# One block for the first feed-forward and the second attention, with waits on the query parts in place of the block's end

## The chip, the core and the metric

The kernel runs on one core of a Trainium2 chip. The metric is the device time of one execution, in microseconds (us). TensorE is called PE, VectorE DVE, ScalarE ACT, GpSimd POOL and SyncE SP, as in the profile. SP computes nothing here; it issues nearly all DMAs.

## What is computed

The reference is a gated cross-attention network of four layers on `x` (2 x 256 rows of 512), each added to `x` through a tanh gate:

```
x = x + tanh(g_xattn[0]) * L0_xattn(layernorm(x), ctx)
x = x + tanh(g_ffn[0])   * L0_ffn(layernorm(x))
x = x + tanh(g_xattn[1]) * L1_xattn(layernorm(x), ctx, ctx)
x = x + tanh(g_ffn[1])   * L1_ffn(layernorm(x))
```

The two layers in the middle matter here. `L0_ffn` is a squared-ReLU feed-forward (512 to 1024 to 512) with a latent expert, routed by the two largest gate logits, and a layernorm behind it. `L1_xattn` is an attention with 32 query heads and 8 key/value heads of dimension 16:

```
q = (query @ Wq) -> 32 heads of 16;  k, v = (ctx @ Wk, ctx @ Wv) -> 8 heads of 16, each for 4 query heads
probs = softmax(q k^T / 4);  out = (probs v) @ Wo
```

## The kernel before

The program is three blocks, one behind the other: the first attention (`attn0`), the first feed-forward (`ffn0`), and the second attention together with the second feed-forward (`attn1`, class `Ffn1`). Each block has one instruction stream per engine, written out by hand; within a block, engines meet at semaphores only. At a block's end every engine waits until all five have come to their end.

`ffn0` (L691 to L1080) also prepares the second attention. Its keys and values come first (`pe_k`, `pe_v`). Its queries come last, at the end of the PE stream: for each batch half `b` the rows of `x` are normalised by DVE (`normalise_1`, L868), transposed by PE, copied to `xnT1` by ACT, and multiplied with `wq1` in four tiles `m` (L1078, 4 matmuls each) into the PSUM banks of `qbank[b][m]`. ACT copies a product's high part to `qpart` (L974) and counts `q_hi`; DVE forms the low part (L895) and counts `q_lo`, from 1 to 8. SP stores both parts of each tile to `q_scratch` in DRAM (L797, 2 DMAs a tile, 16 in all) and, after tile 1 of each half, loads the queries of the first turn back in another layout, 8 DMAs each half (L804), into `a_qS`. The first half's loads count on `stack_in[0]`, the second's on `late_in[0]`. In the second half ACT's copy waits until the first half's tile is stored (`q_out[m]`).

`attn1` (L1317 to L1558) runs over 4 turns `i` of two key heads each, and in each turn over 8 units `m` (batch half times 4 query heads), 32 units in all. For a unit PE does, in two halves:

- scores (L1484): 2 matmuls a half, queries by keys, into three PSUM banks `a_score` in turn. DVE takes the negative maximum of each (L1436, four reduces a unit, `s_max`), and PE waits for the reduce of the bank that it writes next.
- transposed scores (L1495, 4 matmuls), then the negative maxima added by a matmul against a rounded identity `a_ident_r` (L1501, 4 matmuls, which wait for all four maxima of the unit), into `a_scoreT`. ACT takes the exponential (L1405).
- from unit 2 on, in one half of the two, the product with the values (L1517, 16 matmuls) into `a_obank`; every second unit, a small transpose (L1526).

The order on PE is `scores(m+1, 0)`, `scores_T(m, 0)`, product with the values, `scores(m+1, 1)`, `scores_T(m, 1)`. Before the first unit DVE rounds the identity (L1425) and copies the value columns `a_vcol` (`windows`, L1430), which POOL has first set to 0 and 1 (L1393, L1395). Unit 4 (second batch half) waits for `late_in[0]`, unit 8 (turn 1) for `stack_in[1]`. SP loads `wo` (L1372, 4 DMAs), waits for `q_out`, loads turn 1 (L1607 and L1378, 16 DMAs), then the second feed-forward's weights, and turn `i` once turn `i-2` is done.

The PSUM banks: `ffn0` has eight of one bank each, `f_bank0` to `f_bank7`. `attn1` allots `a_score0` to `a_score2` first (banks 0 to 2), then the two `a_scoreT` of two banks each (3 to 6) and `a_obank` (7). The query products of the second half lie in banks 0, 1, 2 and 4, the first half's third in bank 5, the transposes' in 0, 1, 6 and 7:

```
    qbank = [[bank[2], bank[4], bank[5], bank[3]], [bank[0], bank[1], bank[2], bank[4]]]
    tr1_bank = [bank[0], bank[1], bank[6], bank[7]]
```

Of the kernel before, what the change touches and what calls it, by code (L numbers as in the profile page):

```python
# [25 lines left out]
P = 128  # L26
# [23 lines left out]
class Shared:  # L50
    pass

# [638 lines left out]
def ffn0(nc, S, ctx, A):  # L691
# [71 lines left out]
    pe_q, q_hi, q_lo = sem("a_pe_q"), sem("a_q_hi"), sem("a_q_lo")  # L763
# [3 lines left out]
    with nc.Block() as block:  # L767
        @block.sync
        def _(sp):
            def load(c):  # L770
                if c >= 3:
                    sp.wait_ge(w_split, c - 2)
                sp.dma_start(staged(c), chunks[c][1].rearrange("(t p) n -> p t n", p=P)).then_inc(slot_in[c % 3], 16)
            sp.dma_start(gate_stage[:], A.gate_w.rearrange("(t p) n -> p t n", p=P)).then_inc(w_in["gate"], 16)
            for c in range(3):
                load(c)
            sp.dma_start(gamma[:], A.ln_gamma.partition_broadcast(P)).then_inc(w_in["affine"], 16)
            sp.dma_start(beta[:], A.ln_beta.partition_broadcast(P)).then_inc(w_in["affine"], 16)
            for c in range(3, 5):
                load(c)  # L780
            for b in range(B):
                sp.wait_ge(k_lo, b + 1)
                for r in range(2):
                    sp.dma_start(S.k_dram[r, :, b * SC:(b + 1) * SC], f32(S.part[b][:, r, :])).then_inc(S.k_out, 16)
            sp.wait_ge(S.k_out, 64)
            for s in range(2):
                S.load_k(sp, 0, s)
            for c in range(5, len(chunks)):
                load(c)
            sp.wait_ge(w_split, len(chunks))  # L790
            sp.dma_start(S.wqo_stage[:], A.wq1.rearrange("(t p) n -> p t n", p=P)).then_inc(S.wq1_in, 16)
            for b in range(B):
                cols = slice(b * SQ, (b + 1) * SQ)
                for m in range(NQ):
                    sp.wait_ge(q_lo, NQ * b + m + 1)
                    for r in range(2):
                        sp.dma_start(S.q_dram[r, m * P:(m + 1) * P, cols], f32(qpart[:, m, r, :])).then_inc(S.q_out[m], 16)  # L797
                    if m == 1:
                        sp.wait_ge(S.q_out[0], 32 * (b + 1))
                        for s in range(2):  # L800
                            for n in range(4):
                                heads = S.q_dram[n // 2].rearrange("(h d) n -> d h n", d=D1)
                                at = 64 * s + D1 * n
                                sp.dma_start(f32(S.qS[at:at + D1, 0, :, cols]), heads[:, s * GRP:(s + 1) * GRP, cols]  # L804
                                             ).then_inc((S.stack_in, S.late_in)[b][0], 16)

        @block.gpsimd
        def _(pool):
            pool.wait_ge(stats_done, 2 * RT)
            rsqrt_rows(pool, rstd[:], mv[:, :, 1], LN_EPS, S.neg_half[:, 0:RT], rstd_step)  # L810
            pool.wait_ge(gate_split, 1)
            pool.tensor_tensor(gateL[:], gate_stage[:], f32(gateH[:]), ALU.subtract).then_inc(gate_split, 1)
            for c, (_, _, hi, lo) in enumerate(chunks):
                pool.wait_ge(w_hi, c + 1)
                pool.tensor_tensor(lo, staged(c), f32(hi), ALU.subtract).then_inc(w_split, 1)
            for t in range(RT):
                for var, out, done, step in ((mv2, rstd2, stats2_done, rstd2_step),
                                             (S.mv1, S.rstd1, stats3_done, S.rstd1_step)):
                    pool.wait_ge(done, 2 * t + 2)
                    rsqrt_rows(pool, out[:, t:t + 1], var[:, t, 1:2], LN_EPS, S.neg_half[:, 0:1], step, 2 * t)  # L820

        @block.vector
        def _(dve):
            layernorm_stats(dve, S.X, stats, mv, stats_done)
            dve.wait_ge(rstd_step, 2)
            for t in range(RT):
                dve.tensor_scalar(xn[:, t, :], S.X[:, t, :], mv[:, t, 0:1], rstd[:, t:t + 1],
                                  ALU.subtract, ALU.mult).then_inc(xn_done, 1)
            for b in range(B):
                dve.wait_ge(k_hi, b + 1)  # L830
                dve.tensor_tensor(S.part[b][:, 1, :], bank[4 + b][:], f32(S.part[b][:, 0, :]),
                                  ALU.subtract).then_inc(k_lo, 1)
            for t in range(RT):
                dve.wait_ge(xnT_done, t + 1)
                dve.tensor_tensor(xnTL[:, :, t * P:(t + 1) * P], bank[t][:].rearrange("p (k n) -> p k n", k=KT),
                                  f32(xnTH[:, :, t * P:(t + 1) * P]), ALU.subtract).then_inc(xnT_lo, 1)
            for i in range(NL):
                dve.wait_ge(lat_done, i + 1)
                dve.tensor_tensor(latTL[:, i, :], bank[i][:], f32(latTH[:, i, :]), ALU.subtract).then_inc(lat_lo, 1)
            for t in range(RT):  # L840
                dve.wait_ge(logits_done, 1)
                dve.max(top[:, t, :], logits[:, t, :]).then_inc(top_done, 1)
            dve.wait_ge(top_done, RT)
            dve.tensor_tensor(route[:], top[:, :, 0], top[:, :, 1], ALU.add).then_inc(route_done, 1)

            def h_lo_part(i):
                dve.wait_ge(h_hi, i + 1)
                dve.tensor_tensor(hTL[:, i, :], relu[:, i % RT, :], f32(hTH[:, i, :]), ALU.subtract).then_inc(h_lo, 1)
            for i in range(NI):
                dve.wait_ge(relu_done, i + 1)  # L850
                dve.tensor_tensor(relu[:, i % RT, :], relu[:, i % RT, :], relu[:, i % RT, :], ALU.mult).then_inc(h_done, 1)
                if i:
                    h_lo_part(i - 1)
                if i == 1:
                    for e in range(NL):
                        dve.wait_ge(exp_done, e + 1)
                        dve.tensor_tensor(expTL[:, e, :], bank[6 + e][:], f32(expTH[:, e, :]), ALU.subtract).then_inc(exp_lo, 1)
            h_lo_part(NI - 1)
            dve.wait_ge(route_done, 1)
            dve.wait_ge(w_in["affine"], 32)  # L860

            def tile_stats(x, stats_t, mv_t, done, base):
                dve.bn_stats(stats_t, x).then_inc(done, 1)
                dve.wait_ge(done, base + 1)
                dve.bn_aggr(mv_t, stats_t).then_inc(done, 1)
# [783 lines left out]
```

## Time and profile before

| what | us |
|---|---|
| median of 3 runs | 1049.95 |
| lowest and highest of them | 1046.86 and 1050.12 |
| time of the profiled execution | 1048.5 |
| its span in the profile | 1046.7 |
| PE busy | 988.8 (94%) |
| DVE busy | 630.4 (60%) |
| ACT busy | 501.2 (48%) |
| POOL busy | 355.3 (34%) |

The first three rows are times of the whole execution; the span is from the first to the last instruction of the profiled one, 1.8 us less than its time. The profile's times are counted from the span's start. The block of `attn0` lasts to about 755, that of `ffn0` to 857.8, the last to the end. A busy PE is not a PE at its peak, since its matmuls overlap, and their ends are modelled.

### The profile page before, as it was taken

To read this page: it belongs to the slowest core of one execution; us is meant where nothing else is said; L and a number is where in the kernel's file an instruction comes from. 1 tells how busy PE (TensorE), PEld (TensorE's weight loads), DVE (VectorE), ACT (ScalarE), POOL (GpSimd) and SP (SyncE) were. 2 spreads that over 40 slices of the span, in tenths; PEclk is the share of its full clock that TensorE was granted. 3 is DMA by queue.
4 is the path that set the end of the run, shared out by engine and by line. 5 is a ranking of instruction groups with operands and counts; after the bars stand their busy time and mean duration, and the time that the engine had idled before them with its cause. 6 is when DMAs were issued, how large, how long until landed. Compare 5 with 4: busy or idle time off the path is not lost. (4 is left out here: it accounts for less than half of the span.)

```text
span 1046.7 us, 18230 instructions
## 1 busy us (share of the span) xinstructions
PE 988.8 (94%) x6748; PEld 853.7 (82%) x6748; DVE 630.4 (60%) x1102; ACT 501.2 (48%) x968; POOL 355.3 (34%) x244
## 2 busy tenths in 40 slices
PE   4899999999999999999999999999999969999975
PEld 3879989898998989899898989989877757666554
DVE  6566457556646755664675566467448736777464
ACT  4357336535634643563464366346345115556423
POOL 3344324424432442533344153331246203500050
PEclk9989999999999999999999999999999988999987
DMA  6011002001100300110030011000053056430001
GB/s 221 1 62 41 2 1 100 0 0 60 40 0 0 100 0 0 60 40 0 0 100 0 0 60 60 0 0 2 19 194 108 14 167 161 61 61 1 2 0 41
DMA packets 31460, 46.53 MB, mean 44 GB/s; under 512 B 3520, under 2 KB 15424, under 8 KB 31424
## 3 DMA queue, kind: packets, MB, share of 16 engines
q1 hardware_dynamic: 30848, 46.03, 14.8%
q8 instruction: 24, 0.39, 0.2%
q14 instruction: 12, 0.10, 0.0%
q10 hardware_dynamic: 576, 0.00, 0.0%
HBM read 41.83 MB, written 4.19 MB: 44 GB/s over the span
## 5 line engine op out<-in xcount | busy, mean ns | idle before, releaser
L432 DVE TENSOR_TENSOR ptL<-tbank,ptH 128x512 fp32r<-128x512 f32 x192 | 132.1, 688 | 82.7 <-ACT ptH L292 82.5
L292 ACT ACTIVATE ptH<-tbank 128x512 fp32r<-128x512 f32 x192 | 115.6, 602 | 91.2 <-PE tbank L544 90.7
L544 PE MATMUL tbank<-ident,probs 128*128 128x128 f32 x864 | 131.0, 276 | 5.3 <-DVE qTL L434 2.8
L318 ACT ACTIVATE probs<-score,negmax 128x768 f32<-128x768 f32 x128 | 115.5, 903 | 29.7 <-DVE negmax L445 29.7
L445 DVE TENSOR_REDUCE negmax<-score 128x1 f32<-128x768 f32 x128 | 118.8, 948 | 14.6 <-PE score L74 14.6
L72 PE MATMUL obank<-ptH,vH 128*128 128x256 f32 x384 | 121.4, 316 | 0.0
L544 PEld LDWEIGHTS tbank<-ident,probs 128*128 128x128 f32 x864 | 97.8, 140 | 14.5 <-DVE probs L411 3.0
L403 DVE TENSOR_REDUCE sumsq<-probs 128x2 f32<-128x256 f32 (+1 forms) x80 | 42.0, 526 | 112.0 <-ACT probs L287 71.8
L74 PE MATMUL score<-wkvH,kvT_lo 128*128 128x256 f32 x384 | 108.7, 283 | 0.0
L73 PE MATMUL score<-wkvL,kvT_hi 128*128 128x256 f32 x384 | 108.7, 283 | 0.0
L72 PE MATMUL score<-wkvH,kvT_hi 128*128 128x256 f32 x384 | 108.6, 283 | 0.0
L74 PE MATMUL obank<-ptH,vL 128*128 128x256 f32 x384 | 108.4, 282 | 0.0
L73 PE MATMUL obank<-ptL,vH 128*128 128x256 f32 x384 | 108.1, 282 | 0.0
L200 POOL TENSOR_TENSOR rnorm<-sumsq,neg_half 128x2 f32<-128x2 f32 (+1 forms) x80 | 71.4, 895 | 107.1 <-DVE sumsq L405 107.0
L205 POOL TENSOR_TENSOR oTL<-o_norm,oTH 128x512 fp32r<-128x512 f32 x32 | 41.3, 1292 | 187.9 <-ACT oTH L312 187.9
L1436 DVE TENSOR_REDUCE a_negmax<-a_score 128x1 fp32r<-128x512 f32 x128 | 82.1, 684 | 32.5 <-PE a_score L1484 32.0
L72 PE MATMUL score<-kTH,qTH 128*128 128x512 f32 (+1 forms) x256 | 92.8, 363 | 5.8 <-ACT probs L318 4.9
L1405 ACT ACTIVATE a_exp<-a_scoreT 128x1024 f32<-128x1024 f32 x64 | 65.5, 1024 | 62.1 <-PE a_scoreT L1501 62.1
L74 PE MATMUL score<-kTH,qTL 128*128 128x512 f32 (+1 forms) x256 | 87.1, 340 | 0.0
L73 PE MATMUL score<-kTL,qTH 128*128 128x512 f32 (+1 forms) x256 | 86.9, 340 | 0.0
L72 PEld LDWEIGHTS score<-wkvH,kvT_hi 128*128 128x128 f32 x384 | 73.7, 192 | 0.3
L73 PEld LDWEIGHTS score<-wkvL,kvT_hi 128*128 128x128 f32 x384 | 73.7, 192 | 0.3
(257 smaller groups left out, 2320.0 us busy)
## 6 DMA issues: line engine op xcount, KB each, us to landing
wqo_stage<-in_wq SPq DMA_DIRECT2D x9, 1024.0 KB, 5.6
wqo_stage<-in_wo SPq DMA_DIRECT2D x8, 1024.0 KB, 5.0
wkv_stage<-in_wkv SPq DMA_DIRECT2D x9, 512.0 KB, 6.4
a_qS<-q_scratch SPq DMA_DIRECT2D x24, 128.0 KB, 4.9
ctx_stage<-in_ctxT SPq DMA_DIRECT2D x2, 1024.0 KB, 12.8
kS<-k_scratch SPq DMA_DIRECT2D x32, 64.0 KB, 3.3
q_scratch<-qpart SPq DMA_DIRECT2D x16, 128.0 KB, 1.9
wqo_stage<-in_down_w SPq DMA_DIRECT2D x3, 512.0 KB, 3.5
```

Of the source, the lines that this page charges most:

```text
L72: pe.matmul(out, a[0], b[0], start=start, stop=False)
L73: pe.matmul(out, a[0], b[1], start=False, stop=False)
L74: return pe.matmul(out, a[1], b[0], start=False, stop=stop)
L200: pool.tensor_tensor(rn[:, GRP * it:GRP * it + n], ss[:, GRP * it:GRP * it + n], S.neg_half[:, 0:n], ALU.pow).then_inc(rn_done, 1)
L292: act.activation(out, tbank[c % 2][:], ACT.Copy, scale=scale).then_inc(t_hi, 1)
L318: act.activation(probs[:, m % NP, :], score[m % 2][:, 0:SKV], ACT.Exp, bias=negmax[:, m:m + 1], accum_out=rsum[:, m:m + 1]).then_inc(s_exp, 1)
L403: dve.tensor_reduce(ss[:, a:a + n], sq[:, it % 3, 0:n], AX.X, ALU.add).then_inc(ss_done, 1)
L432: i = dve.tensor_tensor(out, tbank[c % 2][:], f32(hi), ALU.subtract)
L445: dve.tensor_reduce(negmax[:, m:m + 1], score[m % 2][:, 0:SKV], AX.X, ALU.max, negate=True).then_inc(s_max, 1)
L544: i = pe.transpose(tbank[c % 2][:, n * P:(n + 1) * P], block_in, S.ident[:])
L1405: act.activation(expo[:, m % NX, h].rearrange("p s k q -> p (s k q)"), scoreT[h][:], ACT.Exp).then_inc(s_exp, 1)
L1436: dve.tensor_reduce(negmax[:, e % 16:e % 16 + 1], score[e % NB][:], AX.X, ALU.max, negate=True).then_inc(s_max, 1)
```

## The change

`ffn0` and `attn1` no longer open a block each. Each returns its five streams, and `flamingo` opens one block in which every engine runs its stream of `ffn0` and then that of `attn1`. The wait of all engines for all at the end of `ffn0` is gone. In its place PE waits for `q_lo` at four places: 3 before its first scores, 6 and 7 before the first use of each `a_scoreT`, 8 before the first product with the values. `attn1`'s PSUM is allotted in another order: `a_scoreT` lie in banks 0 to 3, `a_obank` in 4, `a_score` in 5 to 7. The rounded identity is made by DVE in `ffn0`, after the first layernorm. DVE takes the first four maxima before it copies the value columns instead of after. The memory of `ffn0` in SBUF is still given back before `attn1` takes its own. The diff, without the lines that only moved to another indentation:

```diff
+class Programs:
+    def __init__(self, sync, gpsimd, scalar, vector, tensor):
+        self.sync, self.gpsimd, self.scalar, self.vector, self.tensor = sync, gpsimd, scalar, vector, tensor
...
-    pe_q, q_hi, q_lo = sem("a_pe_q"), sem("a_q_hi"), sem("a_q_lo")
+    pe_q, q_hi, q_lo = sem("a_pe_q"), sem("a_q_hi"), S.q_lo
...
-    with nc.Block() as block:
-        @block.sync
-        def _(sp):
+    def sync(sp):
...
                 dve.tensor_scalar(xn[:, t, :], S.X[:, t, :], mv[:, t, 0:1], rstd[:, t:t + 1],
                                   ALU.subtract, ALU.mult).then_inc(xn_done, 1)
+        dve.tensor_copy(S.ident_r[:], S.ident[:]).then_inc(S.ident_set, 1)
...
+    return Programs(sync, gpsimd, scalar, vector, tensor)
...
-    ident_r = sb("a_ident_r", [P, P], f32r)
...
-    score = [ps(f"a_score{i}", [P, 512], fp32) for i in range(NB)]
     scoreT = [ps(f"a_scoreT{i}", [P, 1024], fp32) for i in range(2)]
     obank = ps("a_obank", [P, 512], fp32)
+    score = [ps(f"a_score{i}", [P, 512], fp32) for i in range(NB)]
...
-            dve.tensor_copy(ident_r[:], S.ident[:]).then_inc(ident_set, 1)
-
...
+        maxima(0)
             dve.wait_ge(ones_set, 1)
             windows(0)
-            maxima(0)
...
                 if m:
                     pe.wait_ge(s_exp, 2 * (m - 1) + h + 1)
+            else:
+                pe.wait_ge(S.q_lo, KT + 2 + h)
...
                     if w:
                         pe.wait_ge(o_step, 2 * w)
+                else:
+                    pe.wait_ge(S.q_lo, 2 * KT)
...
+        pe.wait_ge(S.q_lo, 3)
             for t in range(2):
                 scores(0, t)
-            pe.wait_ge(ident_set, 1)
+        pe.wait_ge(S.ident_set, 1)
...
-            for phase in (ffn0, attn1):
                 with ExitStack() as c:
-                    phase(nc, S, c, A)
+                first = ffn0(nc, S, c, A)
+            with ExitStack() as c:
+                second = attn1(nc, S, c, A)
+                with nc.Block() as block:
+                    @block.sync
+                    def _(sp):
+                        first.sync(sp)
+                        second.sync(sp)
...
```

On PE, from the last query products (`f_bank<-xnT,wqo_stage`) to the first maxima added, before:

```order
L1078 MATMUL f_bank<-xnT,wqo_stage 128x256 x3
L767 UNCONDITIONAL_BRANCH
L1470 UNCONDITIONAL_BRANCH [waits barrier_Pool_Activation_PE_DVE_SP_release]
L1484 MATMUL a_score<-kS,a_qS 128x512 [waits stack_in0]
L1484 MATMUL a_score<-kS,a_qS 128x512 x2
L1484 MATMUL a_score<-kS,a_qS 128x512 [waits a_s_max]
L1484 MATMUL a_score<-kS,a_qS 128x512 [waits a_s_max,a_ident_set]
L1484 MATMUL a_score<-kS,a_qS 128x512 [waits a_s_max]
L1495 MATMUL a_scoreT<-a_qS,kS 128x256 x4
L1501 MATMUL a_scoreT<-a_ident_r,a_negmax 128x2x128 [waits a_s_max]
```

The same place with the change:

```order
L1079 MATMUL f_bank<-xnT,wqo_stage 128x256 x3
L1477 MATMUL a_score<-kS,a_qS 128x512 [waits stack_in0,a_q_lo]
L1477 MATMUL a_score<-kS,a_qS 128x512 x2
L1477 MATMUL a_score<-kS,a_qS 128x512 [waits a_s_max]
L1477 MATMUL a_score<-kS,a_qS 128x512 [waits a_s_max,a_ident_set]
L1477 MATMUL a_score<-kS,a_qS 128x512 [waits a_s_max]
L1490 MATMUL a_scoreT<-a_qS,kS 128x256 [waits a_q_lo]
L1490 MATMUL a_scoreT<-a_qS,kS 128x256 x3
L1496 MATMUL a_scoreT<-ident_r,a_negmax 128x2x128 [waits a_s_max]
```

No matmul has moved or gone; two branches and the wait for all engines have gone, and waits on `a_q_lo` have come.

On DVE in `ffn0`, from the first layernorm's statistics to the low parts of the keys (`part`) and of the normalised rows (`f_xnTL`), before:

```order
L60 BN_AGGR f_mv<-f_stats 128x2 x3
L827 TENSOR_SCALAR f_y<-x_rows,f_mv,f_rstd 128x512 [waits f_rstd_step]
L827 TENSOR_SCALAR f_y<-x_rows,f_mv,f_rstd 128x512 x3
L831 TENSOR_TENSOR part<-f_bank,part 128x512 [waits k_hi] x2
L835 TENSOR_TENSOR f_xnTL<-f_bank,f_xnTH 128x4x128 [waits f_xnT_done] x4
```

The same place with the change:

```order
L66 BN_AGGR f_mv<-f_stats 128x2 x3
L829 TENSOR_SCALAR f_y<-x_rows,f_mv,f_rstd 128x512 [waits f_rstd_step]
L829 TENSOR_SCALAR f_y<-x_rows,f_mv,f_rstd 128x512 x3
L831 CAST ident_r<-ident 128x128
L834 TENSOR_TENSOR part<-f_bank,part 128x512 [waits k_hi] x2
L838 TENSOR_TENSOR f_xnTL<-f_bank,f_xnTH 128x4x128 [waits f_xnT_done] x4
```

The cast has come in front of the keys' low parts.

On DVE between the two phases, from the last layernorm on, before:

```order
L868 TENSOR_SCALAR f_y<-x_rows,mv,rstd 128x512 [waits rstd1_step]
L895 SCALAR_TENSOR_TENSOR qpart<-f_bank,qpart 128x256 [waits a_q_hi] x8
L767 UNCONDITIONAL_BRANCH
L1423 UNCONDITIONAL_BRANCH [waits barrier_Pool_Activation_PE_DVE_SP_release]
L1425 CAST a_ident_r<-ident 128x128
L1430 COPY a_vcol<-v_rows 128x8x16 [waits a_ones_set]
L1430 COPY a_vcol<-v_rows 128x8x16
L1436 TENSOR_REDUCE a_negmax<-a_score 128x1 [waits a_pe_s] x12
```

The same place with the change:

```order
L871 TENSOR_SCALAR f_y<-x_rows,mv,rstd 128x512 [waits rstd1_step]
L898 SCALAR_TENSOR_TENSOR qpart<-f_bank,qpart 128x256 [waits a_q_hi] x8
L1430 TENSOR_REDUCE a_negmax<-a_score 128x1 [waits a_pe_s] x4
L1424 COPY a_vcol<-v_rows 128x8x16 [waits a_ones_set]
L1424 COPY a_vcol<-v_rows 128x8x16
L1430 TENSOR_REDUCE a_negmax<-a_score 128x1 [waits a_pe_s] x8
```

The wait for all engines and the cast are gone from here, and four of the twelve reduces have moved ahead of the copies. On POOL the two memsets of `a_vcol` now follow the last reciprocal root of `ffn0` (L67, L73 with the change) with nothing between, and on SP the loads of `wo` follow the last stores to `q_scratch`.

## Rows read from the trace of the kernel before

**Rows 1.** Who waited for whom, 828 to 872: us in total, times, longest.

```profile
PE a_score L1484 <- PEq L767: 7.1, 1, 7.1
```

**Rows 2.** The timeline of SP, issues only: start, us, line, issue, count.

```profile
843.46 3.62 SPq L804 DMA_DIRECT2D a_qS<-q_scratch  x8
...
851.45 3.86 SPq L804 DMA_DIRECT2D a_qS<-q_scratch  x8
855.36 2.00 SPq L797 DMA_DIRECT2D q_scratch<-qpart  x4
857.75 1.76 SPq L1372 DMA_DIRECT2D a_wo<-in_wo  x4
...
865.18 2.81 SPq L1378 DMA_DIRECT2D a_qS<-q_scratch  x4
```

**Rows 3.** The timeline of all engines, 828 to 872: start, us, instructions, [idle before].

```profile
840.27 0.55 DVE L868 TENSOR_SCALAR f_y<-x_rows,mv,rstd 128x512 f32<-128x512 f32 x1 [1.00 <-POOL rstd L67]
...
841.74 1.04 PE L1071 MATMUL f_bank<-ident,f_y 128*128 128x128 f32 x8
...
843.56 7.14 PE L1078 MATMUL f_bank<-xnT,wqo_stage 128*128 128x256 f32 x32 [0.78 <-issue]
...
851.16 0.42 DVE L895 SCALAR_TENSOR_TENSOR qpart<-f_bank,qpart 128x256 fp32r<-128x256 f32 x1 [0.81 <-ACT qpart L974]
...
857.76 0.95 POOL L1393 MEMSET a_vcol<- 128x1024 f32 x1 [17.52 <-POOLq L767]
...
857.80 1.19 PE L1484 MATMUL a_score<-kS,a_qS 64*128 64x512 f32 x3 [7.09 <-PEq L767]
...
859.23 3.67 DVE L1436 TENSOR_REDUCE a_negmax<-a_score 128x1 fp32r<-128x512 f32 x6
...
862.31 1.22 PE L1501 MATMUL a_scoreT<-a_ident_r,a_negmax 128*128 128x256 f32 x4
```

**Rows 4.** The same view from 870 on, after the clock has risen.

```profile
872.78 0.50 PE L1484 MATMUL a_score<-kS,a_qS 64*128 64x512 f32 x2
...
873.31 2.60 DVE L1436 TENSOR_REDUCE a_negmax<-a_score 128x1 fp32r<-128x512 f32 x4 [1.04 <-PE a_score L1484]
...
874.10 0.50 PE L1484 MATMUL a_score<-kS,a_qS 64*128 64x512 f32 x2
...
889.14 0.50 PE L1484 MATMUL a_score<-kS,a_qS 64*128 64x512 f32 x2
```

**Rows 5.** Issue to landing, first-turn queries (L804), then second-turn queries (L1378).

```profile
DMA to landing us min/median/max: 2.0/2.3/2.3
...
DMA to landing us min/median/max: 4.9/5.6/6.3
```

**Rows 6.** Stretches: us, then PE, PEld, DVE, ACT, POOL busy (count), PE's clock, DMA share, GB/s.

```profile
853.00:854.00 1.00, 0.00 (x0) 0.00 (x0) 0.00 (x0) 0.00 (x0) 0.00 (x0) 0.75 0.48 145
...
870.00:871.00 1.00, 1.00 (x9) 0.70 (x7) 0.47 (x4) 0.53 (x1) 0.00 (x0) 0.71 1.09 166
...
983.00:988.00 5.00, 3.21 (x41) 1.93 (x41) 1.00 (x4) 1.41 (x2) 0.00 (x0) 1.00 0.02 3
...
1007.00:1011.00 4.00, 3.78 (x19) 3.58 (x20) 3.90 (x7) 2.38 (x3) 2.15 (x4) 0.57 0.00 0
```

**Rows 7.** L827 (min/median/max ns), timeline of POOL, DVE, PE from 763 on, then L1425.

```profile
L827 DVE TENSOR_SCALAR f_y<-x_rows,f_mv,f_rstd x4: 539/546/2690, 759.6 to 761.0; 128x512 f32<-128x512 f32 x4
...
763.32 2.59 POOL L815 TENSOR_TENSOR upL<-wqo_stage,upH 128x1024 fp32r<-128x1024 f32 x1
...
763.57 1.27 DVE L831 TENSOR_TENSOR part<-f_bank,part 128x512 fp32r<-128x512 f32 x2
...
768.44 1.29 DVE L835 TENSOR_TENSOR f_xnTL<-f_bank,f_xnTH 128x512 fp32r<-128x512 f32 x2 [2.32 <-ACT f_xnTH L915]
...
769.79 0.39 PE L72 MATMUL f_bank<-f_xnTH,gateH 128*8 128x512 f32 x1 [0.75 <-DVE f_xnTL L835]
...
L1425 DVE CAST a_ident_r<-ident x1: 991/991/991, 857.8 to 857.8; 128x128 fp32r<-128x128 f32 x1
```

More of the change, by code:

```diff
@@ L1341, in attn1 @@
     win = sem("a_win")
-    pe_s, s_max, ident_set = sem("a_pe_s"), sem("a_s_max"), sem("a_ident_set")
+    pe_s, s_max = sem("a_pe_s"), sem("a_s_max")
     pe_sT, s_exp, pe_pv = (sem(f"a_{n}") for n in ("pe_sT", "s_exp", "pe_pv"))
@@ new lines, in sync, with load_q @@
+    def sync(sp):
+        wo_v = A.wo1.rearrange("(i s p r) n -> s p r i n", s=2, p=2, r=P // 4)
+        for s in range(2):
+            for pair in range(2):
+                at = 64 * pair + 32 * s
+                sp.dma_start(wo[at:at + 32, :, :], wo_v[s, pair]).then_inc(wo_in, 16)
+        def load_q(i, s):
+            for n in range(4):
+                heads = S.q_dram[n // 2].rearrange("(h d) n -> d h n", d=D1)
+                at, g = 64 * s + D1 * n, 2 * i + s
+                sp.dma_start(f32(qS[at:at + D1, i % 2, :, :]), heads[:, g * GRP:(g + 1) * GRP, :]).then_inc(stack_in[i % 2], 16)
+        for stored in S.q_out:
+            sp.wait_ge(stored, 64)
+        for i in range(1, TURNS):
+            if i >= 2:
+                sp.wait_ge(pe_sT, 2 * NV * (i - 1))
+            for s in range(2):
+                S.load_k(sp, i, s)
+                load_q(i, s)
+            if i == 1:
+                ffn.loads(sp)
+        ffn.sync(sp)
@@ new lines, in gpsimd, with scalar, exp, copy_o @@
+    def gpsimd(pool):
+        pool.memset(vcol[:], 0.0).then_inc(zeroed, 1)
+        pool.wait_ge(zeroed, 1)
+        pool.memset(vcol[:, :, :, :, D1:D1 + 1], 1.0).then_inc(ones_set, 1)
+        ffn.fold(pool)
+        ffn.gpsimd(pool)
+    def scalar(act):
+        def exp(m, h):
+            act.wait_ge(pe_sT, 2 * m + h + 1)
+            if m >= NX and h == 0:
+                act.wait_ge(pe_pv, (m - NX) // 2 + 1)
+            act.activation(expo[:, m % NX, h].rearrange("p s k q -> p (s k q)"), scoreT[h][:], ACT.Exp).then_inc(s_exp, 1)
+        def copy_o(w):
+            act.wait_ge(pe_pv, w + 1)
+            act.activation(o_quad[:, w % 2, :], obank[:, 0:SQ], ACT.Copy).then_inc(o_copied, 1)
+        for m in range(NM):
+            exp(m, 0)
+            if m % 2 == 1 and m >= 3:
+                copy_o((m - 3) // 2)
+            exp(m, 1)
+        copy_o(NW - 1)
+        for t in range(RT):
+            act.wait_ge(pe_t, t + 1)
+            act.activation(oT[:, :, t * P:(t + 1) * P], score[t % 2][:].rearrange("p (k n) -> p k n", k=KT),
+                           ACT.Copy).then_inc(oT_done, 1)
+        ffn.scalar(act)
@@ L1561, in flamingo @@
+    return Programs(sync, gpsimd, scalar, vector, tensor)
 def flamingo(nc, A):
@@ L1600, in flamingo @@
             S.q_dram = nc.dram_tensor("q_scratch", (2, HEADS * D1, ROWS), fp32, kind="Internal").ap()
+            S.q_lo = sem("a_q_lo")
             S.q_out, S.late_in = [sem(f"q_out{i}") for i in range(KT)], [sem(f"late_in{i}") for i in range(2)]
```

886 lines of the change are left out of this document (423 added, 463 removed).

## The prediction

> **What bounds the kernel now.** I read the busy shares first: PE is busy for 94% of the span, so only time in which PE stands still, or runs at its lower clock, can be won. Then the waits between the two phases. PE's longest wait there is the block's end, 7.1 us, named as PE's own sequencer [rows 1]. The timeline tells who was late. PE's last query product ends at 850.71 (the scores start at 857.80 after 7.09 idle), DVE's last low part at 851.16 + 0.42 = 851.58, and POOL has been idle since 857.76 - 17.52 = 840.24 [rows 3]. SP is last: it issues sixteen stores and sixteen loads of queries one after the other, until 855.36 + 2.00 = 857.36, and 0.4 us later the next block begins with `wo` at 857.75 [rows 2]. So four engines wait for a queue of DMA issues, and of these PE needs only the first half's loads at once.
>
> The wait costs more than itself. In the idle time PE's clock falls (0.75 of full between 853 and 854, that is, from 2.4 to 1.2 GHz within that microsecond) and rises again between 870 and 871 [rows 6]. All that PE does from 857.80 to there runs at 1.2 GHz.
>
> **The change, part by part.** The sum is made against the profiled execution, 1048.5 us, and goes by one landmark: the second scores of unit 3, which start at 872.78, when the clock is full again [rows 4].
>
> *The block's end.* PE goes on with the first scores at about 850.7. Of its two waits `q_lo` >= 3 has long been met, and the queries' loads of the first half are issued by 843.46 + 3.62 = 847.08 [rows 2] and land 2.3 us later at the most [rows 5], at 849.4, with 1.3 us to spare. The maxima then wait for DVE, not for PE: DVE's low parts end at 851.58, where the first reduce took until 859.23 to start [rows 3]. First reduce at 851.6: **7.6 us earlier**. The waits on `q_lo` 6, 7 and 8 are met at 851.58 at the latest, before anything that stands behind them could run.
>
> *The clock, and the order on DVE.* From the first reduce to the landmark it took 872.78 - 859.23 = 13.55 us. At the full clock DVE sets the pace here. Four reduces take 2.60 us [rows 4], 0.65 each; the two copies of `a_vcol` take 859.23 - 857.80 - 0.99 = 0.44 [rows 3, 7]. Before the maxima of unit 2 are all there DVE does twelve reduces and two copies, 12 x 0.65 + 0.44 = 8.2 us, until 859.8. Then PE adds them (half of the 1.32 us that lie between two scores without a product, 872.78 to 874.10 [rows 4], so 0.66) and does the first product with the values. Four units take 889.14 - 874.10 = 15.04 [rows 4], 3.76 each; less two halves of 1.32 that leaves 1.1 for the product. The landmark comes at 859.8 + 0.66 + 1.1 = 861.6, that is 10.0 us after the first reduce: **3.6 us less**. PE alone would need about 1.32 for each of these halves, as much as two reduces, so nothing is gained beyond.
>
> *What lies behind.* From the landmark on the order is unchanged and PE was already the bound; all of it comes 11.2 us earlier if its loads are there. Unit 4 needs the second half's queries: issued by 851.45 + 3.86 = 855.31 [rows 2], landed at 857.6, needed at 874.10 - 11.2 = 862.9. Turn 1's last load is issued by 865.18 + 2.81 = 867.99 [rows 2], 0.4 earlier now since SP never stood still for long, and lands 6.3 us later at the most [rows 5], at 873.9; unit 8 needs it at 889.14 - 11.2 = 877.9. SP's queue now has only 4 us of cover where it had 15.
>
> *The cast in `ffn0`.* It costs DVE's queue between 0 and 2.4 us. Alone it is a short operation, at most the 0.99 us of [rows 7], which the idle time of 2.32 ahead of the last two low parts of the rows takes up. But next to POOL such operations are held: one of the four in front of it took 2690 ns, the others about 540, and the cast's own 0.99 us ended at 858.79 right behind POOL's memset, which ran to 858.71 [rows 7, 3]. POOL's next subtraction starts at 763.32 and runs 2.59 us, to 765.91, and the cast would come at 763.57. Held until then, DVE does its four low parts (1.27 + 1.29) until 768.5 or 768.6 and the last two by 769.9, where they ended at 769.73; PE waits for these at 769.79 [rows 7]. I take the held case, which is the nearest row: **0.2 us more**. Without the 2.32 us of idle time it would be 2.4.
>
> *POOL's memset* moves to 840.24, next to DVE's normalisation at 840.27. Between 0 and 0.95 us for DVE; if that operation ends at 841.8 instead of 840.8, it is still ahead of the second four of PE's eight transposes, which started at 841.74 and take 1.04 [rows 3]; DVE's first low parts and SP's stores then come up to 0.95 later, which leaves 0.3 of the 1.3 us above. I take 0.
>
> *The PSUM banks* cost nothing by themselves: they only decide on which `q_lo` each first write waits. With the old order the first score bank would be that of a late query product.
>
> Sum: 1048.5 - 7.6 - 3.6 + 0.2 = 1037.5. The median of the runs is 1.45 above the profiled time, and the four times average 1048.9; against that average it is 1037.9. I predict **1038.0**.
>
> **The rivals.** (a) *The clock falls all the same.* From 850.7 to the first additions at 854.3 PE does three scores, then waits for a reduce before each of the next ones; with the modelled durations it is busy for some 3 of 3.6 us. Then only the 7.6 us remain, since the 13.55 us stay: 1048.5 - 7.6 + 0.2, about 1041; 1039.5 if the clock comes back within 4 us, as it does after 1007 [rows 6]. For it: the clock can stay low while PE is nearly always busy (3.78 of 4 us at 0.57 there). Against it: between 983 and 988 PE is busy for 3.21 of 5 us in small pieces and keeps the full clock [rows 6]. The Trainium skill warns of this (TensorE: Matmul & The Clock Gate, "A second HAM failure mode: psum-queue depth-cycling"): short idle times between groups of matmuls that go round PSUM banks can make the clock swing between its two levels. By that rule the start of the attention is such a place and the time is the 1041 of this rival; the row of 983 to 988 does not bear it out.
>
> (b) *A load takes the place of the barrier.* Turn 1's loads, with 4 us of cover, or the first half's, with 1.3 or less. If turn 1 landed 10 us after its last issue instead of 6.3 it would cost nothing yet; each microsecond beyond is lost in full. 1039 to 1043, say 1041.
>
> (c) *The change doesn't do what it says*: PE's start stays tied to SP's last stores through one of the counts, and only some tenths are won: about 1048.
>
> (d) *Slower.* The place is the same start of the attention: the clock falls there and stays low. A unit of 3.76 us then takes up to twice that. Four such units beyond the landmark lose 15 us, more than the 11.0 won plus the 0.3% (3.1 us) that a measurement of this kernel can tell from no change; that is where it decides. With six it is 1048.5 - 11.0 + 22.6 = 1060. For it: the clock did stay low for 13 us with PE at work from 857.80 on. Against it: that low stretch began in 7 us of idleness, and once up the clock stays up for the rest of this attention.
>
> **How the numbers follow.** Forecast 0.72; (a) 0.15; (b) 0.06; (c) 0.04; (d) 0.03. The forecast's own range is 1036 to 1039.7: 0 to 0.2 for the cast, 0 to 1 for the memset, and the runs' scatter (1046.86 to 1050.12) halved by taking a median. The range reaches on to (a) and most of (b): **1035.3 to 1042**. Faster by over 0.3%: all of the first three, 0.93. Within 0.3%: (c), 0.04. Slower: 0.03.
>
> **What the profile should show.** PE's wait at its first scores gone or below 0.3 us; the first reduce about 8 us earlier relative to the last query product; a clock of 1.00 from there on; the second scores of unit 3 at about 861.6, give or take what the cast moved; no wait of PE before units 4 and 8; SP's issues in one piece up to turn 1's last. The cast at 763.6, ending near 766.0 if held and at 763.8 if not. From unit 3 to the end the profile should be that of before, moved. The prediction is wrong if the granted clock shows 0.5 after 851, if a DMA ends a wait of PE there, or if the time from unit 3 to the end is longer than the 1046.7 - 872.8 = 173.9 us of before by more than 1 us.

## The result and the profile after

The changed kernel took 1040.32 us (median of nine executions, 1036.86 to 1043.88) beside 1047.18 for the kernel before on the same chip (nine, 1043.36 to 1051.33): a ratio of 0.9923, 95% interval 0.9904 to 0.9942, so 6 to 10 us less. The forecast was 1038.0 in a range of 1035.3 to 1042.0. The profiled execution took 1040.32 too, its span 1038.5, against 1048.5 and 1046.7 before.

First the waits of 828 to 872 after the change (us in total, times, longest). They answer to [rows 1]:

```profile
DVE a_negmax L1430 <- PE a_score L1477: 6.1, 6, 1.9
...
ACT qpart L976 <- DMA q_scratch<-qpart: 3.1, 2, 2.7
...
PE a_score L1477 <- DVE a_negmax L1430: 1.4, 2, 1.2
```

PE's 7.1 us at the block's end are gone. What PE waits for now is DVE's maxima. ACT's copies of the query parts wait for stores of the first half. SP's issues, the same view as [rows 2]:

```profile
842.32 1.81 SPq L801 DMA_DIRECT2D q_scratch<-qpart  x4
844.62 3.62 SPq L808 DMA_DIRECT2D a_qS<-q_scratch  x8
848.29 3.85 SPq L801 DMA_DIRECT2D q_scratch<-qpart  x8
852.61 3.86 SPq L808 DMA_DIRECT2D a_qS<-q_scratch  x8
856.51 3.18 SPq L801 DMA_DIRECT2D q_scratch<-qpart  x4
859.74 1.89 SPq L1371 DMA_DIRECT2D a_wo<-in_wo  x4
...
867.31 1.83 SPq L1377 DMA_DIRECT2D a_qS<-q_scratch  x4
```

SP is still busy until 869.14, in one piece, but nobody waits for its end any more. The timeline of all engines, as [rows 3, 4] (start, us, instructions, [idle before]):

```profile
840.74 0.95 POOL L1391 MEMSET a_vcol<- 128x1024 f32 x1
...
840.82 1.14 DVE L871 TENSOR_SCALAR f_y<-x_rows,mv,rstd 128x512 f32<-128x512 f32 x1 [1.00 <-POOL rstd L73]
...
844.11 7.15 PE L1079 MATMUL f_bank<-xnT,wqo_stage 128*128 128x256 f32 x32 [0.78 <-issue]
...
851.19 0.73 PE L1477 MATMUL a_score<-kS,a_qS 64*128 64x512 f32 x3
...
852.08 0.42 DVE L898 SCALAR_TENSOR_TENSOR qpart<-f_bank,qpart 128x256 fp32r<-128x256 f32 x1 [0.35 <-ACT qpart L976]
852.42 2.47 DVE L1430 TENSOR_REDUCE a_negmax<-a_score 128x1 fp32r<-128x512 f32 x4
...
853.16 0.50 PE L1477 MATMUL a_score<-kS,a_qS 64*128 64x512 f32 x1 [1.24 <-DVE a_negmax L1430]
...
853.85 1.00 PE L1477 MATMUL a_score<-kS,a_qS 64*128 64x512 f32 x2 [0.19 <-DVE a_negmax L1430]
...
855.02 1.02 PE L1496 MATMUL a_scoreT<-ident_r,a_negmax 128*128 128x256 f32 x4
...
866.31 0.50 PE L1477 MATMUL a_score<-kS,a_qS 64*128 64x512 f32 x2
...
882.69 0.50 PE L1477 MATMUL a_score<-kS,a_qS 64*128 64x512 f32 x2
```

The scores follow the last query product without a pause. The first reduce starts at 852.42, right behind DVE's last low part. But unit 3's second scores come at 866.31 and not at 861.6. The stretches say why, as [rows 6] (PE, PEld, DVE, ACT, POOL busy, then PE's granted clock):

```profile
852.00:853.00 1.00, 0.00 (x0) 0.00 (x0) 0.92 (x2) 0.05 (x1) 0.00 (x0) 1.00 0.80 273
...
855.00:856.00 1.00, 1.00 (x7) 0.76 (x6) 1.00 (x4) 0.00 (x0) 0.00 (x0) 0.64 0.44 136
860.00:861.00 1.00, 1.00 (x5) 0.78 (x6) 0.39 (x1) 0.32 (x1) 0.00 (x0) 0.50 0.69 203
...
865.00:866.00 1.00, 1.00 (x16) 0.44 (x16) 0.00 (x0) 0.72 (x1) 0.00 (x0) 0.74 1.14 234
```

PE pauses from 851.92 to 853.16, the clock falls to its lower level, 1.2 GHz, between 855 and 856, and is back between 865 and 866. In this execution rival (a) came true.

To compare profiles, whose first feed-forwards start up to 2.6 us apart, I count from the second half's first query product (843.56 before, 844.11 after):

| from ... to | before | after | difference |
|---|---|---|---|
| start of the profile, second half's products | 843.56 | 844.11 | +0.55 |
| ... first reduce | 15.67 | 8.31 | -7.36 |
| ... unit 3's second scores | 13.55 | 13.89 | +0.34 |
| ... first product with `wo` | 117.48 | 116.80 | -0.68 |
| ... end of the span | 56.44 | 55.39 | -1.05 |

The block's end gave its 7.4 us, and the clock's 3.6 us are missing. The last two rows are scatter and no work of the change (over all fourteen profiles they go from 116.8 to 118.2 and from 54.2 to 57.3): in the profile before, PE waits 0.7 us for a copy of the value columns at about 902, and PE is at the lower clock for 25 us in all behind 1000, beside 21 us after.

But nine executions reach from 1036.9 to 1043.9, and they go with the mean granted clock: five at 0.984 or less took 1040.3 to 1043.9, four at 0.986 or more 1036.9 to 1039.1. So the clock may fall in some executions of one and the same program and not in others. That became the question.

The mean clock is a coarse measure for it. Each profile also has low stretches elsewhere, at about 50 to 60 and behind 995. Added up over the span, microsecond by microsecond, PE is at the lower clock at the attention's start and elsewhere for:

| profile | at the start, us | elsewhere, us | mean clock |
|---|---|---|---|
| before | 17 | 31 | 0.978 |
| the change | 10 | 25 | 0.984 |
| change_again | 14 | 32 | 0.979 |
| last_low_part_awaited | 7 | 21 | 0.988 |
| memset_after_normalisation | 0 | 32 | 0.986 |
| one_block_filled | 0 | 27 | 0.988 |

Over all fourteen profiles "elsewhere" goes from 21 to 35 us. By an estimate from these rows that alone makes mean clocks from about 0.984 to 0.991, with nothing at the start. So by this range executions at 0.983 or less fell at the start; from 0.984 to 0.988 the mean doesn't tell.

### The profile page after: what moved, and what is told of

The parts are those of the page before. It is cut to its first block and busy times, and to the rows that moved or that the text cites. A ratio compares the mean times of both kernels' runs of the same rounds, so it can differ in the third digit from the quotient of the medians.

```text
span 1038.5 us, 18220 instructions
## 1 busy us (share of the span) xinstructions
PE 986.1 (95%) x6748; PEld 851.2 (82%) x6748; DVE 628.2 (60%) x1102; ACT 501.7 (48%) x968; POOL 355.5 (34%) x244
```

## The experiments

All twelve in one table. "First reduce" and "to unit 3" are the second and third line of the table above; "pause" is PE's longest between its last query product and the first additions; the last column counts executions at a mean clock of 0.985 or less, and in brackets those at 0.983 or less. The ratio is to the kernel before, run in between on the same chip.

| run | first reduce | to unit 3 | pause | clock low | median us (runs) | ratio, 95% interval | at 0.985 or less |
|---|---|---|---|---|---|---|---|
| before | 15.67 | 13.55 | 7.09 | 853-871 | 1047.18 (9) | 1 | – |
| the change | 8.31 | 13.89 | 1.24 | 855-866 | 1040.32 (9) | 0.9923 (0.9904-0.9942) | 5 (4) |
| change_again | 8.23 | 15.07 | 1.17 | 854-869 | 1041.53 (6) | 0.9907 (0.9878-0.9936) | 4 (3) |
| one_block_filled | 8.28 | 10.82 | none | never | 1037.91 (6) | 0.9906 (0.9883-0.9929) | 0 (0) |
| block_end_filled | 16.28 | 14.89 | 1.47 | 861-875 | 1050.18 (12) | 1.0023 (1.0008-1.0037) | 12 (11) |
| memset_after_normalisation | 7.94 | 9.67 | 0.87 | never | 1038.47 (6) | 0.9910 (0.9890-0.9930) | 0 (0) |
| old_banks | 8.28 | 9.68 | 1.04 | never | 1039.43 (6) | 0.9922 (0.9904-0.9939) | 3 (1) |
| order_alone | 14.97 | 12.09 | 7.02 | 853-867 | 1047.89 (12) | 0.9991 (0.9979-1.0003) | 12 (12) |
| copies_first | 8.51 | 15.15 | 1.45 | 853-868 | 1041.17 (6) | 0.9921 (0.9905-0.9937) | 4 (4) |
| filled_and_late_memset | 7.94 | 11.16 | none | never | 1037.90 (4) | 0.9888 (0.9869-0.9906) | 0 (0) |
| stores_awaited | 16.61 | 11.61 | 8.66 | 855-870 | 1050.99 (12) | 1.0029 (1.0014-1.0043) | 12 (12) |
| last_low_part_awaited | 8.92 | 12.47 | 1.24 | 854-862 | 1040.17 (6) | 0.9928 (0.9909-0.9948) | 3 (2) |
| few_fillers_late_memset | 7.94 | 10.05 | none | never | 1037.01 (4) | 0.9891 (0.9867-0.9914) | 0 (0) |
| memset_after_normalisation_2 | 7.93 | 9.68 | 0.87 | never | 1037.49 (6) | 0.9902 (0.9877-0.9927) | 1 (1) |

**PE kept busy at the attention's start (one_block_filled).** Ten matmuls of the identity and the keys, whose result is overwritten, stand in PE's pauses; the first scores wait for one more query part, and PE's wait for the rounded identity moves ahead of them:

```diff
+        def fill(n):
+            for _ in range(n):
+                pe.matmul(scoreT[1][:, 512:1024], S.ident_r[:, :], kS[:, 0, 0:512], start=True, stop=True)
...
                 if e >= NB:
+                    fill({3: 5, 4: 2, 5: 2}.get(e, 0))
                     pe.wait_ge(s_max, e - NB + 1)
...
+            if m == 0 and h == 0:
+                fill(1)
             pe.wait_ge(s_max, 4 * m + 4)
...
-        pe.wait_ge(S.q_lo, 3)
+        pe.wait_ge(S.q_lo, 4)
```

> The changed kernel with ten matmuls more (128 rows, 512 columns, results not used), which PE does where it otherwise waits for the first maxima: five, two, two and one. Pauses theory: the clock falls at 855.6 in the changed kernel because PE stands still for some 1.2 and 0.2 us between 851.9 and 853.9; with the pauses filled the granted clock stays 1.00 from 851 on, the second scores of unit 3 come about 10.0 us after the first reduce instead of 13.9, and the kernel is 3 to 4 us faster than the changed one (ratio to before about 0.989). Rival theory: the clock falls by what the attention's start itself does (its half-row matmuls), pauses or not; then it falls again, the 13.9 us stay, and the ratio stays near 0.992 or is worse by the added matmuls.

The timeline of PE and two stretches of this run:

```profile
851.78 1.42 PE L1469 MATMUL a_scoreT<-kS,ident_r 128*128 128x512 f32 x5
...
863.15 0.50 PE L1484 MATMUL a_score<-kS,a_qS 64*128 64x512 f32 x2
```

```profile
852.00:853.00 1.00, 1.00 (x5) 0.64 (x4) 1.00 (x3) 0.00 (x0) 0.00 (x0) 1.00 0.78 266
...
856.00:866.00 10.00, 10.00 (x86) 7.36 (x89) 8.13 (x15) 6.24 (x7) 0.00 (x0) 1.00 0.85 203
```

The same matmuls as with the change and ten more, no pause, and the clock stays at its upper level, 2.4 GHz; no execution lies below 0.987. With what the two later versions with fillers show, the fall comes from PE's pauses here. The fillers also delay the additions (from the query products to them 12.25 us instead of 10.91 with the change), so that the start takes 10.82 and not 10.0. The 3 to 4 us that were expected in time did not show: the ratio, 0.9906, can't be told from the change's, 0.9923 and 0.9907.

**PE kept busy up to the block's end (block_end_filled).** The kernel before, with thirty matmuls that nobody reads behind the last query product:

```diff
+            pe.wait_ge(q_lo, 3)
+            for _ in range(30):
+                pe.matmul(bank[5][:], hTH[:, 0, 0:P], downH[:, 0, :], start=True, stop=True)
```

> The kernel before, with the block's end and its 7 us of waiting kept, but PE does 30 unused matmuls (128 rows, 512 columns, about 6.9 us) before it comes to the end. Measures the clock's part alone. Pauses theory: the clock stays at 1.00, or falls later in the attention's start as in the changed kernel; if it stays, 3.5 us are won with the barrier in place (ratio about 0.9967). Rival theory (the attention's start brings it down): the clock is 1.00 until about 861 and then falls; then well under 2 us are won.

```profile
850.91 7.22 PE L1083 MATMUL f_bank<-downH,kvT_hi 128*128 128x512 f32 x30
858.97 0.70 PE L1487 MATMUL a_score<-kS,a_qS 64*128 64x512 f32 x3 [0.84 <-PEq L767]
861.13 1.99 PE L1487 MATMUL a_score<-kS,a_qS 64*128 64x512 f32 x3 [1.47 <-DVE a_negmax L1439]
```

```profile
860.00:861.00 1.00, 0.00 (x0) 0.00 (x0) 0.88 (x4) 0.00 (x0) 0.09 (x1) 1.00 0.90 260
861.00:862.00 1.00, 0.86 (x2) 0.48 (x2) 1.00 (x3) 0.00 (x0) 0.00 (x0) 0.59 1.14 248
```

The wait at the block's end is down to 0.84 us, the clock outlives it, and then falls behind the pause of 1.47 us. The time is no better than before, 1 to 4 us worse; in the profile the first reduce comes 0.6 us later, and the start takes 1.3 us longer, since its low stretch began later and lasted until 875. The idle time at the block's end was thus enough to drop the clock but not needed for it: the pauses behind it do the same.

**POOL's memset after the normalisation**, twice:

```diff
                 rsqrt_rows(pool, out[:, t:t + 1], var[:, t, 1:2], LN_EPS, S.neg_half[:, 0:1], step, 2 * t)
+        pool.wait_ge(q_lo, 4)
```

> The changed kernel, but POOL waits for q_lo 4 before it clears a_vcol, so that the memset no longer runs beside DVE's last normalisation (1.14 us there, 0.55 before). Theory that the memset held it: the normalisation takes 0.55 again, the stores and the first reduce come 0.6 us earlier relative to the query products, the kernel is 0.3 to 0.6 us faster than the changed one, more only if the clock is spared. Rival: the 0.6 us lie beside other work, the first reduce comes no earlier.

> The memset after the query parts, once more and with more runs. Theory (with DVE 0.3 us earlier at the start of the scores PE's pause is 0.87 instead of 1.24 us, and the clock stays up): again no run at a mean clock below 0.985, and 1037 to 1039. Rival (the clock's fall is chance there too and was missed by luck in six runs): single runs at 0.982 and 1041 to 1043.

DVE's and then PE's timeline in the second of them:

```profile
840.41 0.55 DVE L872 TENSOR_SCALAR f_y<-x_rows,mv,rstd 128x512 f32<-128x512 f32 x1 [1.00 <-POOL rstd L73]
```

```profile
852.38 0.49 PE L1478 MATMUL a_score<-kS,a_qS 64*128 64x512 f32 x1 [0.87 <-DVE a_negmax L1431]
...
861.32 0.50 PE L1478 MATMUL a_score<-kS,a_qS 64*128 64x512 f32 x2
```

DVE's normalisation is back at 0.55 us, where it took 1.14 beside the memset. The first reduce comes 0.37 us earlier, and PE's pause is 0.87 instead of 1.24. With the clock up, the start takes 9.67 and 9.68 us: the forecast's 10.0. Both profiles keep the clock, and eleven of twelve executions are at 0.986 or more. One is not (0.983, 1042.49), so the expectation that none would be was wrong: with the shorter pause the fall was rarer, and not excluded. The time can't be told from the change's (ratios 0.9910 and 0.9902), though 0.3 to 0.6 us were expected, which is less than these runs can tell.

**The old order of the PSUM banks**, in one block, with the waits that it needs:

```diff
+    score = [ps(f"a_score{i}", [P, 512], fp32) for i in range(NB)]
     scoreT = [ps(f"a_scoreT{i}", [P, 1024], fp32) for i in range(2)]
     obank = ps("a_obank", [P, 512], fp32)
-    score = [ps(f"a_score{i}", [P, 512], fp32) for i in range(NB)]
...
+                else:
+                    pe.wait_ge(S.q_lo, KT + 1 + e)
...
-                pe.wait_ge(S.q_lo, KT + 2 + h)
+                pe.wait_ge(S.q_lo, 2 * KT)
```

> The changed kernel with the PSUM allotment of before (scores in banks 0 to 2), so the first three scores wait for q_lo 5, 6 and 7 and the transposed ones for 8. Theory that DVE sets the pace: the first reduce starts when DVE has done its last low part, whichever bank the scores use, so the time is that of the changed kernel within 0.5 us (ratio 0.992). Rival theory that the banks matter: PE starts its third score only at about 851.8 and everything behind it comes up to 1 us later; more if the longer pause brings the clock down earlier.

The first scores start 7.08 us after the query products in both orders, and the ratio is the same. The allotment is worth nothing that can be measured.

**The change once more**, beside the three that follow, so that its mix of clocks is known better:

> The changed kernel as it is, once more, beside the others of this group. Theory (the clock falls at the start of the attention in about half of the executions, and each fall costs 4 us): its runs fall into two groups, at mean clocks of about 0.982 and 0.987, some 4 us apart, and the ratio to before is again 0.991 to 0.994. Rival (the two groups of the first time were scatter of the whole program): the times lie close together, or don't go with the clock. In the profile, if the low stretch is there, the time from DVE's first reduce to the second scores of unit 3 is about 13.9 us, and without it about 9.7.

Two groups again: four at 0.979 to 0.985 with 1040.8 to 1043.5, two at 0.988 and 0.991 with 1037.5 and 1033.3. Of fifteen executions of the change, nine are in the group of the lower clock (median 1042.27 us), seven of them at 0.983 or less, and six in the other (1037.47 us). The two sets ran beside kernels before of 1047.18 and 1049.39, so the medians of the pooled groups are good to a microsecond or two. In the profile the low stretch is there, and the start took 15.07 and not the 13.9 expected of it: the stretch lasted 14 us here and 10 the first time.

**The order on DVE and the cast alone**, with the block's end kept:

```diff
+            dve.tensor_copy(S.ident_r[:], S.ident[:]).then_inc(S.ident_set, 1)
             for b in range(B):
...
-            dve.tensor_copy(ident_r[:], S.ident[:]).then_inc(ident_set, 1)
...
+            maxima(0)
             dve.wait_ge(ones_set, 1)
             windows(0)
-            maxima(0)
```

> The kernel before with its block end, but with the cast in the first feed-forward and the maxima ahead of the copies of the value columns. Theory: DVE's first reduce comes up to 1.2 us earlier after the block's end (the cast's 0.99 and the copies' 0.44 no longer stand ahead of it), but the clock is at its low level there and PE is what is slow, so the second scores of unit 3 come at most 1 us earlier; time 0 to 1.2 us below before, ratio 0.999 to 1.000. Rival (DVE's order sets the pace of the start even at the low clock): 1.2 us or more, and the first additions move by as much as the first reduce.

0.9 us less, within an interval of 2.2 less to 0.3 more, so the time lies where the theory put it, and no gain is shown. In the profile the first reduce and the first additions each came 0.7 us earlier, as the rival has it. Unit 3's second scores came 2.2 us earlier and not at most 1; this execution, the fastest of the twelve, had its clock back at 867 and not at 871, so the profile doesn't price the order. The run bounds what these two edits bring while the block's end stands.

**The copies of the value columns ahead of the maxima**, in one block:

```diff
-        maxima(0)
         dve.wait_ge(ones_set, 1)
         windows(0)
+        maxima(0)
```

> One block, but DVE copies the value columns before the first four maxima, as before the change. Theory (what PE's pauses at the start are like decides on the clock): the first reduce comes 0.4 us later and PE's first pause is longer; the clock falls in at least as many executions as with the change, 1040 to 1043 us. If the order matters to nothing but DVE's own 0.44 us: the change's time and the same mix of clocks. By the prediction's sum, where DVE sets the pace and does twelve reduces and two copies in either order, it costs nothing at all.

The first reduce comes 0.2 to 0.3 us later than in the two profiles of the change, and PE's pause grows to 1.45. The time can't be told from the change's (0.9921 beside 0.9907), and four of six executions are at 0.983 or less, beside seven of fifteen with the change. The order of the copies decides nothing that shows.

**PE alone waits for SP's last stores:**

```diff
         pe.wait_ge(S.q_lo, 3)
+        pe.wait_ge(S.q_out[3], 64)
```

> One block, but PE alone waits before its first scores until both halves of the last query tile are stored (q_out[3] at 64), which SP issues last; no other engine waits. Theory (of the block's end only SP's queue cost anything): PE idles 7 to 9 us, since here it waits for the landing and not for the issue, the first scores start 15 to 17 us after the first query product and all of the gain is gone, 1047 to 1051, with the clock low in every run. Rival (waking five engines, entering a new block or its code was part of the price): 2 us or more of the gain stay, 1043 to 1046.

```profile
858.42 1.98 SPq L801 DMA_DIRECT2D q_scratch<-qpart  x4
...
861.89 1.19 PE L1477 MATMUL a_score<-kS,a_qS 64*128 64x512 f32 x3 [8.66 <-issue]
...
862.69 2.48 DVE L1430 TENSOR_REDUCE a_negmax<-a_score 128x1 fp32r<-128x512 f32 x4 [8.28 <-PE a_score L1477]
```

In one block, and everything is lost again: 1.5 to 4.5 us slower than before. The stores are issued by 860.40 and PE starts 1.49 us later, at 861.89, since it waits for the landing, where the block's end waited for the issue. In the profile before, PE started 0.44 us after SP's last issue (857.36 to 857.80). So entering a block, its branches and its code can have cost 0.44 us at most; the rest of the 7.1 was SP's queue.

**PE waits for the last query part:**

```diff
-        pe.wait_ge(S.q_lo, 3)
+        pe.wait_ge(S.q_lo, 2 * KT)
```

> One block, but PE's first scores wait for the eighth query part instead of the third. PE pauses for about 0.9 us after its last query product; the first reduce comes about 0.5 us later, since DVE was busy until then anyway. Theory (a longer pause ahead of the scores lets the clock fall): low in nearly all runs, mean clocks at or below 0.983, 1041 to 1044. Rival (the fall comes from the short pauses among the scores or from elsewhere, and not from this pause): the same mix as with the change and 0.5 us on top, about 1041 with single runs at 1037.

```profile
851.91 0.73 PE L1477 MATMUL a_score<-kS,a_qS 64*128 64x512 f32 x3 [1.24 <-DVE qpart L898]
853.19 0.50 PE L1477 MATMUL a_score<-kS,a_qS 64*128 64x512 f32 x1 [0.55 <-DVE a_negmax L1430]
```

PE's pause now stands ahead of the scores, 1.24 us, with 0.55 behind them. The theory (low in nearly all runs) was wrong: three of six executions are at 0.986 or more and two at 0.983 or less, a mix like the change's, as the rival had it. The profiled one, at 0.988, has a low stretch all the same, from 854 to 862 only, and little of it elsewhere. A mean clock of 0.986 or more doesn't say that the clock stayed up at the start.

**Fillers and the later memset together**, the edits of both runs together, first with ten fillers, then with five:

```diff
-                    fill({3: 5, 4: 2, 5: 2}.get(e, 0))
+                    fill({3: 3, 4: 1, 5: 1}.get(e, 0))
...
-                fill(1)
```

> One block, POOL's memset after the last query part, and eight matmuls that nobody reads in the pauses of PE's first scores and one more before the first additions, while the first scores wait for the fourth query part instead of the third. What each part did alone should hold together: no low clock in any run, the query parts 0.3 to 0.6 us earlier as with the memset moved, but the additions some 1.1 us later as with the fillers. Theory (fillers only help by keeping the clock, which the memset's place keeps as well): no gain over the memset moved alone, 1037 to 1038.5. Rival (both gains add up): below 1036.5.

> As the run with fillers and the memset moved, but with five fillers instead of ten, placed only where PE paused with the memset moved (0.87 and 0.19 us). Theory: the clock stays up and the additions are no longer delayed; first reduce to the second scores of unit 3 9.7 to 10.2 us instead of 11.2, and 1036 to 1037.5. Rival (with fewer fillers the clock falls in some runs): single runs at 1041 and a mean clock of 0.982 in them.

```profile
854.78 0.73 PE L1506 MATMUL a_scoreT<-ident_r,a_negmax 128*128 128x256 f32 x4
...
861.73 0.50 PE L1485 MATMUL a_score<-kS,a_qS 64*128 64x512 f32 x2
```

With ten the start takes 11.16 us, with five 10.05, both as expected. Ten brought 1037.90 us, which is the theory's time (no gain over the memset moved alone) and not the rival's. No execution of the eight, nor of the fourteen with fillers in all, lies below 0.986, where nine of fifteen of the change do, seven at 0.983 or less; and all three profiles with fillers keep the clock at the start, where both of the change lose it. The version with five fillers had 1037.01 beside 1048.83, within 1.9 us from end to end. Against the change it is 2 to 3 us lower by the ratios (0.9891 beside 0.9923 and 0.9907), but their intervals overlap, so as a gain in time this is likely and not shown; that fillers keep the clock up here is.

## Why the prediction was right, point by point

The number was right, and the block's end with it. The forecast's second part, the clock, did not happen in the profiled execution, which is also the median: its granted clock shows 0.5 after 851, which the prediction itself had named as a sign of being wrong. The median lies inside the range because the range reached on to rival (a), and close to the forecast because both cases occur.

**The block's end (7.6 us): right**, measured 7.36. The missing quarter of a microsecond is the memset's (below). stores_awaited shows the cause as the prediction had it, SP's queue of issues. The loads of the first half were there in time: issued by 848.24, scores at 851.19 without a pause.

**The clock and the order on DVE (3.6 us): the mechanism right, its chance wrong.** With the clock up DVE sets the pace as the sum had it: 9.67 to 9.68 us in three profiles, forecast 10.0 (four reduces take 2.47 here and not 2.60). The step that failed is the weight of rival (a), 0.15. It was set low because PE was taken to be busy "for some 3 of 3.6 us" before the additions. In the profile it is busy for 2.3 of 3.8: of 851.26 to 855.02, 1.24 + 0.19 us are pauses, and in the microsecond from 852 PE does nothing at all. The prediction gives no row for the 3; in the profile three of the score matmuls run at once, in 0.73 us, and the next waits for the first reduce. The row of 983 to 988, which was held against the rival, has pauses of 0.67, 0.50 and 0.62 us and none of over a microsecond, and did not carry over. What (a) said of the cost was about right: its 1041 stands beside 1042.27, the forecast's 1038 beside 1037.47, the medians of the two groups, of which a part is low stretches elsewhere. The measured median, 1040.32, lies between them since both occur.

The Trainium skill's page TensorE: Matmul & The Clock Gate, under "A second HAM failure mode: psum-queue depth-cycling", blames short idle times between groups of matmuls for such swings. By the row of 852 to 853 and the fillers, which took away the pauses and with them the fall, the runs agree with it in this place.

**The cast (0.2): it cost nothing, held or not.** The profile of the change, DVE and POOL:

```profile
760.13 1.92 DVE L829 TENSOR_SCALAR f_y<-x_rows,f_mv,f_rstd 128x512 f32<-128x512 f32 x4 [1.48 <-POOL f_rstd L73]
...
761.96 0.22 DVE L831 CAST ident_r<-ident 128x128 fp32r<-128x128 f32 x1
...
764.46 2.41 POOL L818 TENSOR_TENSOR upL<-wqo_stage,upH 128x1024 fp32r<-128x1024 f32 x1
```

None of the four before it was held here, the cast ran in 0.22 us, and POOL's long subtraction came 2.5 us later. But in one_block_filled it was held, just as the prediction had it, and so in two more of the twelve profiles with the cast in this place (stores_awaited, few_fillers_late_memset):

```profile
763.77 2.57 POOL L818 TENSOR_TENSOR upL<-wqo_stage,upH 128x1024 fp32r<-128x1024 f32 x1
...
764.01 2.41 DVE L831 CAST ident_r<-ident 128x128 fp32r<-128x128 f32 x1
```

It goes with which of the two engines starts first. In the four profiles in which one of the four normalisations was held (before and these three), POOL's first subtraction starts 5.58 to 5.74 us after DVE's first statistics, in the ten others 5.78 to 6.34. And even the 2.4 us cost nothing: in all fourteen profiles the second half's first query product comes 88.30 to 88.37 us after these statistics. In one_block_filled DVE's last low parts end 14.49 us after them, before 14.51, so the idle time ahead of them took the cast up whole, and the sum's 0.2 was rounding and no cost.

**The memset (0, bound 0.95): mis-sized, 0.37 within its bound.** DVE's normalisation took 1.14 us beside it, 0.55 without; PE's transposes did not come later for it, as the prediction said, but SP's stores and ACT's last copies did. That is 0.37 us at the first reduce, by the runs with the memset moved, and a longer pause of PE with it. The Trainium skill, SBUF — State Buffer, "SBUF: two separate sides", has GpSimd and certain DVE operations (one in a 2-port perf mode, for one) take turns at a port pair, for a whole instruction each, whichever starts first; the 1.14 beside 0.55, behind a memset that started 0.08 us earlier, agrees with it.

**The banks (0): right**, by old_banks. **What lies behind: right.** PE waits nowhere before unit 4 or unit 8; turn 1's last load is issued by 869.14, and unit 8's first scores are at 882.69. **Rivals (b), (c), (d):** no load took the barrier's place, the tie to SP is gone, and no low stretch outlasted the start: in the one-block profiles without an added wait on SP the latest ends at 869, before unit 4.

What stays open: why the clock falls in some executions of the same program and not in others. In the one-block profiles without fillers the longest pause was 1.17 to 1.45 us where the clock fell, and 0.87 or 1.04 where it stayed, but no boundary follows from that: old_banks, 1.04 in its profile, also had an execution at 0.981, and the memset moved one at 0.983. The length of the low stretch at the start differs too, from 7 to 14 us in one block. What else differs from execution to execution no run here shows.

## What to carry to other kernels

A block's end costs what its last engine's queue costs, here SP's DMA issues, and hardly more (0.44 us at most here): look in the timeline for who comes last, and let each engine wait only for what it reads. After taking a long wait away, list the pauses that stay behind it, each by itself, before counting on the clock: a pause of a microsecond ahead of the steady part can drop it as well, and here about half of the executions lost what was won. Don't settle it by one profile, nor by the mean clock alone where there are low stretches elsewhere. Where such a pause can't go, a few matmuls whose result is overwritten held the clock here, but only as many as fit in the pause; each one beyond delays the work.

## What the runs showed of the hardware

One and the same program fell into two groups some 5 us apart (1042.27 and 1037.47), for the most part by whether PE's clock fell in one place of a millisecond. The low stretch began behind pauses of PE and lasted 7 to 14 us in one block, though PE was busy without a gap in it (1.00 of the microsecond from 860 on, at 0.50 of the clock). By the profiles a low stretch of 7 us costs 2.8 us (12.47 less 9.68), one of 10 us 4.2 (13.89) and one of 14 us 5.4 (15.07): 0.4 us for each, less than half, since at the upper level DVE and not PE sets the pace.

DVE's operations beside POOL's were held in some executions of the same program and not in others: a cast of 128x128 took 0.22 us in nine profiles and 2.4 in three, and it went with the start of a subtraction on POOL: 5.58 to 5.74 us after DVE's first statistics where DVE was held, 5.78 to 6.34 where it was not.
